# SyncE's queue: the transposes of u ahead of the last two stores and of the second half of the load

## What is computed

```python
# layer 0: linear attention on a group norm of x, four heads of 32 channels
xn = gn(x) / norm_over_channels * g * C ** 0.5          # this is u
q, k, v = split(einsum('bchw,oc->bohw', xn, w_qkv))     # k and v with 4 memory columns in front
q = softmax(q, over the 32 channels of a head) * scale
k = softmax(k, over the pixels)
x = x + w_out @ (context(k, v) applied to q) + b_out
# layer 1: a 3x3 convolution masked to (j - i) % 4 == 0, and a 1x1 one for the other pairs
x = x + conv3x3(gn(x), w3 masked) + w1 masked @ gn(x) + b.sum(1)
```

## Time and profile before

| | us |
|---|---|
| median of 3 runs | 1960.87 |
| lowest, highest | 1960.73, 1961.2 |
| the profiled execution's own time | 1962.26 |
| its span, first to last instruction | 1960.5 |
| TensorE busy | 1861.5 (95%) |
| VectorE busy | 1632.6 (83%) |
| ScalarE busy | 1369.6 (70%) |
| GpSimd busy | 1311.3 (67%) |
| DMA queue of SyncE, share of 16 DMA engines | 75.3% |

### The profile page before, as it was taken

One profiled execution on the slowest core, in us unless ns is written; L12 is line 12 of the kernel. 1 busy time (PEld: TensorE's weight loads), 2 busy tenths in 40 slices (PEclk: granted clock), 3 DMA queues, 4 the chain that ended last, 5 costly groups with the idle time before them and its releaser, 6 DMA issues.

```text
span 1960.5 us, 51383 instructions
## 1 busy us (share of the span) xinstructions
PE 1861.5 (95%) x21521; PEld 993.2 (51%) x21521; DVE 1632.6 (83%) x3108; ACT 1369.6 (70%) x1480; POOL 1311.3 (67%) x729
## 2 busy tenths in 40 slices
PE   3799999999999999999999999999999999999997
PEld 1455554555554555544555544555544555544552
DVE  6778888888888788888888888888888888888874
ACT  4677776776776777766777766777676777766761
POOL 6476767686666676767676767676667686667670
PEclk8989999999999999999999999999999999999999
DMA  6267877887877797877788878787877797877765
GB/s 130 46 139 157 178 165 155 169 176 160 171 164 161 150 180 157 178 164 159 162 181 152 178 162 157 163 181 150 180 160 161 157 182 156 177 165 157 156 145 145
DMA packets 349430, 313.01 MB, mean 160 GB/s; under 512 B 299152, under 2 KB 299920, under 8 KB 341008
## 3 DMA queue, kind: packets, MB, share of 16 engines
q1 hardware_dynamic: 346656, 305.75, 75.3%
q10 hardware_dynamic: 2224, 3.97, 0.8%
q0 software_dynamic: 320, 0.01, 0.0%
HBM read 68.10 MB, written 67.11 MB: 69 GB/s over the span
## 4 chain that ended last, share of the span: by engine, by line
PE 54%; SPq 21%; DVE 18%; DMA 4%; issue 2%; ACT 1%; POOL 0%; ACTq 0%; DVEq 0%; POOLq 0%
PE pair_ps L922 18%; PE pair_ps L904 8%; DVE km L1286 7%; SPq L334 6%; SPq L321 5%; PE pair_ps L913 5%; PE pair_ps L863 4%; SPq L333 4%; DVE u L1283 4%; DVE image L1338 4%; PE pair_ps L885 3%; PE bank_ps L814 3%; DMA replicas<-yg_lo 3%; PE pair_ps L823 3%; SPq L306 2%; SPq L327 2%
## 5 line engine op out<-in xcount | busy, mean ns | idle before, releaser
L922 PE MATMUL pair_ps<-replicas,w_rep 96*32 96x512 f16 x8192 | 490.3, 383 | 18.0 <-DMA replicas<-yg_lo 18.0
L489 POOL TENSOR_TENSOR u_lo<-u,u_hi 128x1024 f16<-128x1024 f32 x128 | 269.9, 2139 | 280.2 <-ACT u_hi L608 280.2
L492 POOL TENSOR_TENSOR exp_kT_lo<-exp_kT,exp_kT_hi 128x1024 f16<-128x1024 f32 x128 | 273.1, 2134 | 192.8 <-ACT exp_kT_hi L620 190.2
L922 PEld LDWEIGHTS pair_ps<-replicas,w_rep 96*32 96x32 f16 x8192 | 201.6, 96 | 279.8 <-issue 76.7
L495 POOL TENSOR_TENSOR u_lo<-exp_q,u_hi 128x1024 f16<-128x1024 f32 x128 | 270.4, 2142 | 25.7 <-ACT u_hi L626 25.2
L608 ACT ACTIVATE u_hi<-u 128x1024 f16<-128x1024 f32 x128 | 135.3, 1057 | 144.5 <-DVE u L1283 137.5
L1338 DVE SCALAR_TENSOR_TENSOR image<-pair_ps,image 128x512 f32<-128x512 f32 x256 | 175.5, 686 | 45.3 <-PE pair_ps L922 41.3
L626 ACT ACTIVATE u_hi<-exp_q 128x1024 f16<-128x1024 f32 x128 | 131.5, 1050 | 109.2 <-DVE exp_q L1325 109.0
L485 POOL TENSOR_SCALAR u<-image,st 128x1024 f32<-128x1024 f32 x128 | 179.3, 1409 | 29.4 <-DVE st L1222 29.4
L863 PE MATMUL pair_ps<-wqk_hi,u_hi 128*128 128x128 f16 x1024 | 181.5, 222 | 0.0
L1325 DVE TENSOR_TENSOR exp_q<-exp_q,pair_ps 128x1024 f32<-128x1024 f32 x128 | 152.9, 1216 | 32.8 <-PE pair_ps L823 29.8
(11 more groups left out here) (184 smaller groups left out, 4500.2 us busy)
## 6 DMA issues: line engine op xcount, KB each, us to landing
image<-in_x SPq DMA_DIRECT2D x256, 256.0 KB, 4.8
out<-image SPq DMA_DIRECT2D x502, 128.0 KB, 2.3
replicas<-yg_hi SPq DMA_DIRECT2D x252, 165.0 KB, 3.7
replicas<-yg_hi SPq DMA_DIRECT2D x252, 107.2 KB, 2.4
replicas<-yg_lo SPq DMA_DIRECT2D x126, 165.0 KB, 4.2
replicas<-yg_lo SPq DMA_DIRECT2D x126, 107.2 KB, 2.3
uT_hi<-u_hi SPq DMA_TRANSPOSE x128, 4.4
uT_lo<-u_lo SPq DMA_TRANSPOSE x128, 4.0
```

The source lines that it names most:

```text
L489: pool.tensor_tensor(px(UL, v), px(U, v), px(UH, v), ALU.subtract).then_inc(ul_ready, 1)
L492: pool.tensor_tensor(KL[:, v % 2], KT[:, v % 2], KH[:, v % 2], ALU.subtract).then_inc(kl_ready, 1)
L922: mm = pe.matmul(conv_ps[32 * r:32 * r + 32, j % 2], w_rep[0:32 * SLOTS, tap, r], rep[:, j * ROWS + dy:(j + 1) * ROWS + dy, dx:dx + SIDE], ...
```

## The change

In SyncE's `step` three things move. The transposes of unit 0 come ahead of the third store group (`store(e, 2)`); those of units 1 and 2 come ahead of the fourth (`store(e, 3)`), which before stood ahead of unit 1; and those of unit 3 (with those of unit 2) come ahead of the second half of the load. Besides, pairs of waits that stand together ahead of one instruction change places, in SyncE's and in TensorE's `step`.

```diff
@@ SyncE's step @@
                 if p is not None and p >= PRELOADED:
                     if e is not None:
+                        sp.wait_ge(stored[1], at(e, 16 * RES, 16 * RES))
+                    if e is not None:
                         sp.wait_ge(stored[0], at(e, 16 * RES, 16 * RES))
-                    if e is not None:
-                        sp.wait_ge(stored[1], at(e, 16 * RES, 16 * RES))
                     load(p, 0)
+                if a is not None:
+                    sp.wait_ge(ul_ready, at(a, UNITS, 1))
+                    turn_u(a, 0)
                 if e is not None:
                     sp.wait_ge(out_ready, at(e, CHUNKS, 6))
                     store(e, 2)
                 if a is not None:
-                    sp.wait_ge(ul_ready, at(a, UNITS, 1))
-                    turn_u(a, 0)
+                    sp.wait_ge(ul_ready, at(a, UNITS, 2))
+                    turn_u(a, 1)
+                    sp.wait_ge(ul_ready, at(a, UNITS, 3))
+                    turn_u(a, 2)
                 if e is not None:
                     sp.wait_ge(out_ready, at(e, CHUNKS, 8))
                     store(e, 3)
                 if a is not None:
-                    sp.wait_ge(ul_ready, at(a, UNITS, 2))
-                    turn_u(a, 1)
+                    sp.wait_ge(ul_ready, at(a, UNITS, 4))
+                    turn_u(a, 3)
                 if p is not None and p >= PRELOADED:
...
                     load(p, 1)
-                if a is not None:
-                    sp.wait_ge(ul_ready, at(a, UNITS, 3))
-                    turn_u(a, 2)
-                    sp.wait_ge(ul_ready, at(a, UNITS, 4))
-                    turn_u(a, 3)
                 if c is not None:
                     sp.wait_ge(hi_ready, at(c, UNITS, 2))
                     replicate_high(c, 0)
+                    sp.wait_ge(lo_odd, at(c, UNITS // 2, 1))
                     sp.wait_ge(lo_even, at(c, UNITS // 2, 1))
-                    sp.wait_ge(lo_odd, at(c, UNITS // 2, 1))
                     replicate_low(c, 0)
@@ TensorE's step, one of seven such pairs @@
+                    pe.wait_ge(uT_in[2], at(a, 32, 32))
                     pe.wait_ge(kl_ready, at(a, UNITS, 3))
-                    pe.wait_ge(uT_in[2], at(a, 32, 32))
                     context(a, 2, bank_ps[0])
```

More of the change, by code:

```diff
@@ L985, in step @@
                     rough_q(a, 1, pair_ps[0])
+                    pe.wait_ge(k_max, at(a, 8, 8))
                     pe.wait_ge(ul_ready, at(a, UNITS, 1))
-                    pe.wait_ge(k_max, at(a, 8, 8))
                     keys(a, 0, pair_ps[2])
@@ L1005, in step @@
                     keys(a, 3, pair_ps[0])
+                    pe.wait_ge(kl_ready, at(a, UNITS, 1))
                     pe.wait_ge(uT_in[0], at(a, 32, 32))
-                    pe.wait_ge(kl_ready, at(a, UNITS, 1))
                     context(a, 0, bank_ps[0])
@@ L1010, in step @@
                     turn_q_max(bank_ps[1])
+                    pe.wait_ge(uT_in[1], at(a, 32, 32))
                     pe.wait_ge(kl_ready, at(a, UNITS, 2))
-                    pe.wait_ge(uT_in[1], at(a, 32, 32))
                     context(a, 1, bank_ps[0])
@@ L1036, in step @@
                     denominators(a, 3, bank_ps[1])
+                    pe.wait_ge(uT_in[3], at(a, 32, 32))
                     pe.wait_ge(kl_ready, at(a, UNITS, 4))
-                    pe.wait_ge(uT_in[3], at(a, 32, 32))
                     context(a, 3, bank_ps[0])
@@ L1096, in step @@
                 if c is not None:
+                    pe.wait_ge(hi_in[1], at(c, 16 * 2 * RES, 16 * 2 * RES))
                     pe.wait_ge(lo_in[1], at(c, 16 * RES, 16 * RES))
-                    pe.wait_ge(hi_in[1], at(c, 16 * 2 * RES, 16 * 2 * RES))
                     conv_ring(c, 3)
```

## The result

| | before | changed |
|---|---|---|
| median of 4 runs, us | 1961.03 | 2029.57 |
| lowest, highest | 1960.73, 1966.91 | 2017.55, 2041.52 |
| the profiled execution's own time | 1962.26 | 2031.57 |
| its span | 1960.5 | 2029.8 |
| mean granted clock of TensorE | 0.989 | 0.978 |

The changed kernel is slower: the ratio is 1.0342, with a 95% interval of 1.0277 to 1.0407. That is 68.5 us, where 15 were forecast. The sign was right and the size was not: 2029.6 lies above the range, which ended at 2005. The four runs of the changed kernel lie unusually far apart, and their time goes with the clock: 2017.55 at 0.983, 2027.57 at 0.979, 2031.57 at 0.978, 2041.52 at 0.975. That is the first hint of a part of the loss that the forecast left out.

The account below looks back on a forecast made before the run. SyncE's in-order queue, delaying replicas for TensorE, was taken to bound each step; 34.8 us of new group-means waits less 19.7 of gains gave +15.1 on 1960.87, so 1976.0 us, range 1941 to 2005.

Parts of the forecast that it names:

- The bound: Ring-to-ring step of 58.1 us plus TensorE's wait; SyncE's queue makes yg_lo replicas late, 18.0 us in 21 waits.
- The replicas: Replicas of yg_lo, ahead of TensorE's ring: land at 1012.4, asked for at 1014.5; all 18.0 us given back.
- Rival D: SyncE's queue reaches the replicas only after some 1002, so they stay late; given no time of its own.
- The term of 1.7 us for the clock at 662: TensorE's ring matmuls after the 2.00 us wait at 662.27 ran at granted clock 0.50; 1.7 us more gained.
- The swapped waits: Swapped wait pairs in SyncE and TensorE ask for the same values before the same instruction: costed at nothing.
- The mechanism of the loss: Load's second half starts 3.4 us later; VectorE's statistics, then TensorE's group means wait once it lands after about 1004.6.
- the size of the wait: TensorE ahead of the group means: 1.2 us a step in 29 steps, 34.8 us; ends no wait and 3.2.
- The start: SyncE's second half of the load, behind four turns and two store groups: starts at 998.2 (996.4 to 999.0).
- The duration: Second half of the load, first issue to last landing: taken as 7.6 us, ends 6.9 and 8.8.
- Rival C: Waits of 2 us or more at TensorE's group means also lower the clock, 1.7 us each: 2010 us; chance 0.07.
- A: SyncE's queue doesn't stall, the load lands at 1003.3, before 1004.6; only gains remain: 1941.2 us; chance 0.30.
- B: A draw: load lands at 1005.3 on average, group-means waits cancel the gains: 1961 us; chance 0.10.

Follow-up runs that it names:

- the order with the load at 39.3: Against the load-one-turn-earlier order (L0 T0 S2 T1 T2 S3 L1 T3), the last stores also one turn earlier (L0 T0 S2 T1 S3 T2 L1 T3): 1944.29 us, ratio 0.9899.
- two of the orders between, with the load at 41.0 and 41.5: Load's second half behind unit 2's transposes, against before: 1964.05 us, 1.0005; load ahead of unit 3's transposes, against the changed kernel: 1967.31 us, 1.0012.

## Why the prediction was right and wrong

**The bound, right.** The queue of SyncE sets both waits, and each shortens or lengthens the span in full; the order alone moved the time from 0.990 to 1.073 of the kernel before.

**The replicas, right.** Forecast: the wait of 18.0 us goes, the low ones land at 56.1 after the ring's start, 2 us ahead of TensorE. Measured: they land at 56.65, and in the 29 steps the wait is gone. That the number holds to the tenth is luck. I took all 21 waits for one place in 31 steps; 20 of them, 16.7 us, stood there, and as differences of starts they happen to come to 18.0. The 21st, 1.3 us at the end of the program, stayed and became 2.7. Rival D, the replicas late still, fell with it. The term of 1.7 us for the clock at 662 went too, but in a sum with 21.1 on the other side it means nothing.

**The swapped waits, right.** Costed at nothing; 1.0015, with 1 inside the interval.

**The mechanism of the loss, right.** The load's second half, the statistics, the group means, in this order; the deadline of 1004.6 (48.3 after the ring) held to a tenth of a microsecond in the table above. VectorE's wait was forecast at 2.7 us a step and is 110.9 / 29 = 3.8, longer by about the 1.0 by which the landing is later than forecast.

**The first failed step: the size of the wait, 1.2 us forecast, 2.23 measured.** Two terms of it were each half a microsecond short. The start: turn 0 begins 25.78 after the ring, as walked (982.1 is 25.8), but from there to the load it took 16.65 on the average, for 14.3 + 1.8 = 16.1. I had given stalls to the turns alone. The eight transposes took 11.74 for 10.5 by their rows, and the rest, two store groups and the gaps, some 4.9 for 3.8: stalls fall on stores too, as on the 3.12 above. The load started at 42.43, for 41.9. The duration: 8.08 for the 7.6 that I took, inside the bounds of 6.9 and 8.8; the other orders show 7.2 to 7.9, and what makes it longest in the changed kernel wasn't tried. Together 1.2 + 0.5 + 0.5 = 2.2. In time: 64.6 instead of 34.8, and this alone would have given 1960.9 + 64.6 - 19.7 = 2006, the upper end of the range. A mean wait of 2.2 had been the range's own edge; with two terms that fail in the same direction on a deadline, it should have reached on to the 3.2 that the ends of the terms gave, 29 x 3.2 - 19.7 = +73.

**The second failed step: the clock, left out.** Rival C had the mechanism and 0.07 of the chance. It said that a wait of 2 us or more may cost 1.7 us, and that a wait of 1.74 lost nothing, from two rows. Measured, 12 of 29 waits lost 1.6 to 2.8 us each, 22 us in all; C's own number, 10 steps of 1.7 on a mean wait of 1.8, was 2010. The guess of 2 us was nearly right as a floor: no wait below 1.87 lost anything, and waits of 1.89, 1.95 and 1.99 lost 1.7 each. By their rows, the count of the 1.74 that C was held against, these three are 1.73, 1.78 and 1.83: a wait as long as the harmless one did lose the clock. And C was judged by the forecast's mean wait of 1.2. The waits scatter from 0.8 to 3.9, and where the forecast's mean is near such a floor, a part of the steps is always beyond it. The clock belonged into the forecast as a term, not beside it as a rival.

With both steps put right the sum closes, in us of span: 15.1 forecast, 29.8 more of waits at the group means, 22.8 of clock (21.1 lost where 1.7 was to be gained) and the rest of 1.6 come to 69.3.

**Rivals A and B.** A, the load in time and 1941.2 us, fell in the changed kernel: its premise, the load at 40.1 after the ring by a queue without stalls, was nowhere seen; the earliest of the 29 starts at 41.4. Its time is real all the same: the order with the load at 39.3 comes to 1944.29, with both gains and no loss. The figure of the Trainium skill ("DMA: Bandwidth & Descriptors", Latency and other measured facts) for a transpose's rate, by which A would have held, isn't what the queue paid: a transpose of 256 KB held it for 11.74 / 8 = 1.47 us on the average here, which would be 178 GB/s. B, the draw, fell as well, though two of the orders between, with the load at 41.0 and 41.5, are just that draw. The same page's rule to issue early and wait late (Rules for kernel authors) agrees with the table: between a load at 41.0 and one at 44.1 the ratio goes from 1.0005 to 1.0734.

## What to carry to other kernels

In an in-order DMA queue a transfer's place is a budget: write down for each the time at which its reader asks, its landing and the slack, and move another past it only as long as the slack of the load (here 48.3 less 45.7, 2.6 us, a little less than the 3.0 by which one turn moved it) covers it. A reordering may give its gain by one move and its loss by another, so try the moves apart: here turns 0 to 2 one place forward won 1%, turn 2 ahead of the last stores as well gave that back, and turn 3 ahead of the load lost over 3%. Cost a new idle time of TensorE at more than its length once some of the waits pass some 1.9 us, and look at the granted clock behind them.

## What the runs showed of the hardware

- The clock's fall doesn't follow the length of a wait alone. In the changed kernel waits of 1.89, 1.95 and 1.99 us at the group means lost 1.7 us each, and waits of 2.78, 2.86, 3.25 and 3.56 lost nothing, with the same work before and behind them (3.40 and 3.76 by the rows above are 3.56 and 3.93 here). What decides between them stays open.
- Matmuls that nobody reads, in place of an idle time, made a kernel faster than the same one without them: by 48.6 us with 16 of them a step (1.0734 to 1.0509), by some 14 with 8.
- The second transpose behind the load holds the queue some 2.2 us longer than any other: 3.78 us at 583.49 above, and 3.5 to 4.0 on the average in the kernel before and in the four orders where a turn follows the load, for 1.2 to 1.8 on the average elsewhere. The replicas in that place are not held so: eight took 5.58 behind the load at 603.51, and 5.95 at 587.31 behind a turn. So the change saved this stall as well, ahead of the replicas, which I had not counted. What the transpose waits for wasn't tried.
